# A 16-chunk mixer and expert kernel on one core: softmax, merge and scan of chunk 0 one unit down, weight pieces awaited one by one, chunk 1's x1 made in one step

## The chip, the cores and the metric

The kernel runs on 1 core of one Trainium2 chip. The metric is the device time of one execution in microseconds (us). Three runs of the kernel before took 1112.18, 1112.43 and 1113.23 us; the median is 1112.43 us.

## The reference

The input has 16 sequences of 512 tokens with 128 features. Everything is float32. With LN as a layer norm without weights:

```
x = x + LN(attn(LN(x)))            # attn: a diagonal state space model, 64 states
x = x + LN(ffn(LN(x)))             # ffn: 8 experts, all of them run for every token

attn(u):  Bu = u @ B_w.T
          h  = causal convolution of Bu with the powers of 64 eigenvalues of modulus 1
          y  = h @ C_w.T + D * u
ffn(x):   cw = softmax(x @ w_router) * softmax(x @ w_gating / 0.1), normed over the experts
          out = sum over e of cw[e] * ((silu(x @ w_gate[e]) * (x @ w_up[e])) @ w_down[e])   # F = 512
```

## The kernel before

**Tiling.** One sequence is a chunk. Its expert work is cut into 32 units `k`: unit `k` is block `b = k % 4` (128 of the 512 hidden features) of expert `e = k // 4`. For a unit TensorE makes `g` and `u` (gate and up), ScalarE the silu `gate` and a rounded copy `hid_hi`, VectorE the product `hid`, and VectorE or GpSimd the rest `hid_lo = hid - hid_hi` (GpSimd for `k % 4` in 1 and 3). Four units later TensorE makes the down product `y`. Each product is three matmuls on split numbers (high by high, high by low, low by high; function `exact`), so a unit is nine matmuls of 128x512. After an expert's fourth down product VectorE multiplies `y` by the weights of the tokens, `cw_b` (`weigh`, L1127), and GpSimd adds the parts (`add_part`).

**Order.** Each engine runs its own list of instructions in the order written. What an engine does beside a unit stands in tables (L44 to L58) that give the unit after which a step comes: `FIRST_X_AT` and `FIRST_Y_AT` are the steps that prepare chunk 1 inside chunk 0, `SECOND_X_AT` those for chunk 2, and `FIRST_OWN_AT` the softmax of chunk 0's own router. From chunk 1 on the tables `X_AT`, `Y_AT` and `OWN_AT` hold; the change leaves them alone.

**The mixer in chunk 0.** For chunk 1 the steps are: `lo_x` (`act_lo`, VectorE), `bu` (two matmuls into `m_ps`), `merge`, `enter_cos`, `enter_sin`, `scan` (a running sum over 512 tokens), `leave`, `fold`, `lo_w` (all VectorE), `c` (two matmuls), `y`, `turn_y` (four transposes on TensorE into `n_ps`), `stats_y`, `var_y`, then `z` and the residual, the second norm (`stats_x1`, `var_x1`, `scale_x1`), `turn_xe`, `lo_xe` and the router's `logits`.

**Waits around the change.** `u` of unit k waits for `hid` of unit k-2 (L506). The down product of expert 2, at unit 12, writes the `y` buffer of expert 0 and waits until `weigh` of expert 0 has read it (L520). `weigh` of expert 0 stands at unit 10 and needs `cw_b`, which comes by two DMAs from the last step of the softmax (`weights`, unit 6).

**Weights.** The 8 experts' weights come as three pieces each (gate, up, down; 24 pieces numbered n = 3e + i) into one of two stage slots, by SyncE's DMAs. ScalarE rounds a piece to `w_hi` (`round_piece`), and the rest `w_lo` is made for pieces 0 to 8 by TensorE and ScalarE before the loop (`make_lo`, `keep_lo`), for pieces 9 to 23 by GpSimd inside chunk 0 (`split_piece`) at the units in `LATE_SPLITS`. A slot is loaded again when all three pieces of the expert in it are split, and ScalarE waits for all three DMAs of an expert before it rounds the first piece. TensorE waits before an expert's first unit for all its three pieces.

Of the kernel before, what the change touches and what calls it, by code (L numbers as in the profile page):

```python
# [39 lines left out]
AHEAD = 3  # L40
PIECES = WCOLS // F

# [15 lines left out]
FIRST_OWN_AT = {"softmax": 1, "peak": 2, "silus": 3, "exps": 4, "products": 5, "weights": 6, "weigh": 10}  # L58
# [20 lines left out]
LATE_SPLITS = (3, 4, 5, 6, 7, 8, 9, 10, 11, 13, 14, 15, 19, 21, 22)  # L79
# [25 lines left out]
def build(nc, x_in, proj_in, angles_in, d_in, wgate_in, wup_in, wdown_in, out):  # L105
# [13 lines left out]
    with ExitStack() as ctx:  # L119
# [49 lines left out]
        y_shift = sb("y_shift", [P, NT])  # L169
# [20 lines left out]
        w_loaded = [sem("w_loaded0"), sem("w_loaded1")]  # L190
# [57 lines left out]
        def _(sp):  # L248
# [4 lines left out]

            def load_expert(e):
# [96 lines left out]
            for e in range(2, AHEAD):  # L351
                load_expert(e)
            load_expert(AHEAD)
            load_expert(AHEAD + 1)

            def body(c, par, first, last):
                if c + 2 < NCHUNK:
                    load_x(c + 2)
                if first:
                    load_expert(AHEAD + 2)  # L360
                store_cw(c, par)
                for e in range(E):
# [4 lines left out]
                    if e == 3 and first:  # L367
                        load_expert(AHEAD + 3)
# [3 lines left out]
                    if e == 5 and first:  # L372
                        load_expert(AHEAD + 4)
# [19 lines left out]
        def _(pe):  # L393
# [103 lines left out]

            def gate_up(c, par, k, first):
                e, b, buf = k // NB, k % NB, k % 2
                if first and b == 0:  # L500
                    if e < AHEAD:
                        pe.wait_ge(w_lo_act, PIECES * (e + 1))
                    else:
                        pe.wait_ge(w_lo_done, PIECES * (e + 1 - AHEAD))
# [7 lines left out]
            def down(c, k, first):  # L512
# [95 lines left out]
            def body(c, par, first, last):  # L608
                for k in range(UNITS):
# [991 lines left out]
```

## Time and profile before

| what | value |
|---|---|
| median of three runs | 1112.43 us |
| the profiled execution | 1113.27 us |
| its span in the trace | 1111.4 us |
| TensorE (PE) busy | 1094.8 us, 99% of the span |
| VectorE (DVE) busy | 941.4 us, 85% |
| ScalarE (ACT) busy | 744.6 us, 67% |
| GpSimd (POOL) busy | 719.2 us, 65% |
| chain that ended last | PE 88% of the span |

Times are counted from the span's start. PE is TensorE's matmuls and PEld its weight loads, DVE is VectorE, ACT ScalarE, POOL GpSimd, and SPq the queue on which SyncE issues DMAs. The loop over units starts at 26.54 us, chunk 1 at about 101 us. Successive matmuls overlap in the records, so the step between two starts, not the duration, is what one costs: 0.23 us for 128x512.

### The profile page before, as it was taken

The page shows a single profiled execution, that of the slowest core. Times are in us where ns is not written, and L with a number is a line of the kernel's source. Part 1 is how long each engine was busy: PE and PEld are TensorE (multiplying, and loading weights), DVE is VectorE, ACT ScalarE, POOL GpSimd, SP SyncE. Part 2 cuts the span into 40 slices and gives each one's busy share as a digit, 9 for nine tenths or more (in the row PEclk, how much of TensorE's full clock was granted, in tenths as well). Part 3 has the DMA queues.
Part 4 walks back from the last instruction along what each step waited for, and adds up shares of the span by engine and source line. Part 5 has one row for each costly group of instructions (what it writes and reads, how often), then busy time and mean ns, then how long its engine had stood idle before and what let it go on. Part 6 is the DMA issues. An engine that isn't in the chain of part 4 may idle for free.

```text
span 1111.4 us, 16965 instructions
## 1 busy us (share of the span) xinstructions
PE 1094.8 (99%) x4833; PEld 896.1 (81%) x4833; DVE 941.4 (85%) x1815; ACT 744.6 (67%) x1435; POOL 719.2 (65%) x886
## 2 busy tenths in 40 slices
PE   8899999999999999999999999999999999999997
PEld 5777888888888888888888888888888888888886
DVE  7999898897988979788897988979788897987866
ACT  5786676757667586676757667586676757666553
POOL 2785766748567575766748567575766748556454
PEclk9999999999999999999999999999999999999999
DMA  4430413313142221413213142221313213131110
GB/s 138 132 87 9 117 48 96 76 35 100 39 105 66 73 74 36 115 48 96 76 32 103 39 105 67 71 76 43 107 48 96 76 32 102 39 95 48 47 50 20
DMA packets 182285, 79.66 MB, mean 72 GB/s; under 512 B 124560, under 2 KB 160048, under 8 KB 182192
## 3 DMA queue, kind: packets, MB, share of 16 engines
q1 hardware_dynamic: 182192, 78.57, 26.5%
q8 instruction: 40, 0.66, 0.2%
q14 instruction: 53, 0.43, 0.1%
HBM read 59.14 MB, written 19.40 MB: 71 GB/s over the span
## 4 chain that ended last, share of the span: by engine, by line
PE 88%; issue 0%; POOL 0%; DVE 0%; POOLq 0%; ACT 0%; DVEq 0%; ACTq 0%
PE u L396 10%; PE g L397 10%; PE g L396 10%; PE u L397 10%; PE y L397 10%; PE y L396 10%; PE g L398 10%; PE u L398 10%; PE y L398 10%; PE n_ps L485 0%; PE n_ps L486 0%; PE m_ps L464 0%; PE m_ps L463 0%; PE m_ps L457 0%; PE m_ps L458 0%
## 5 line engine op out<-in xcount | busy, mean ns | idle before, releaser
L1500 POOL TENSOR_TENSOR hid_lo<-hid,hid_hi 128x512 fp32r<-128x512 f32 x256 | 341.0, 1332 | 306.6 <-ACT hid_hi L781 306.1
L775 ACT ACTIVATE gate<-g 128x512 f32<-128x512 f32 x512 | 306.0, 598 | 313.6 <-PE g L398 312.8
L1115 DVE TENSOR_TENSOR hid<-gate,u 128x512 f32<-128x512 f32 x512 | 348.0, 680 | 145.7 <-ACT gate L775 110.0
L781 ACT ACTIVATE hid_hi<-hid 128x512 fp32r<-128x512 f32 x512 | 319.6, 624 | 20.0 <-DVE hid L1115 19.3
L1124 DVE TENSOR_TENSOR hid_lo<-hid,hid_hi 128x512 fp32r<-128x512 f32 x256 | 218.4, 853 | 0.2
L396 PE MATMUL u<-xe_hi,w_hi 128*128 128x512 f32 (+1 forms) x516 | 201.0, 389 | 2.9 <-DVE hid L1115 2.7
L396 PE MATMUL g<-xe_hi,w_hi 128*128 128x512 f32 (+1 forms) x516 | 200.4, 388 | 0.3 <-DVE xe_lo L1251 0.3
L397 PE MATMUL g<-xe_lo,w_hi 128*128 128x512 f32 (+1 forms) x516 | 200.1, 388 | 0.0
L397 PE MATMUL u<-xe_lo,w_hi 128*128 128x512 f32 (+1 forms) x516 | 200.0, 388 | 0.0
L398 PE MATMUL u<-xe_hi,w_lo 128*128 128x512 f32 (+1 forms) x516 | 199.9, 387 | 0.0
L398 PE MATMUL g<-xe_hi,w_lo 128*128 128x512 f32 (+1 forms) x516 | 199.9, 387 | 0.0
L396 PE MATMUL y<-hid_hi,w_hi 128*128 128x512 f32 (+1 forms) x516 | 199.6, 387 | 0.0
L397 PE MATMUL y<-hid_lo,w_hi 128*128 128x512 f32 (+1 forms) x516 | 199.5, 387 | 0.0
L398 PE MATMUL y<-hid_hi,w_lo 128*128 128x512 f32 (+1 forms) x516 | 199.4, 387 | 0.0
L1507 POOL TENSOR_TENSOR acc<-acc,y_part 128x512 f32<-128x512 f32 x110 | 143.5, 1305 | 27.2 <-DVE y_part L1133 25.6
L396 PEld LDWEIGHTS u<-xe_hi,w_hi 128*128 128x128 f32 x516 | 96.9, 188 | 26.2 <-DVE hid L1115 6.5
L396 PEld LDWEIGHTS g<-xe_hi,w_hi 128*128 128x128 f32 x516 | 96.9, 188 | 20.9 <-ACT w_lo L658 0.9
L396 PEld LDWEIGHTS y<-hid_hi,w_hi 128*128 128x128 f32 x516 | 96.9, 188 | 20.3
L398 PEld LDWEIGHTS u<-xe_hi,w_lo 128*128 128x128 f32 x516 | 96.9, 188 | 20.0
L398 PEld LDWEIGHTS g<-xe_hi,w_lo 128*128 128x128 f32 x516 | 96.9, 188 | 19.9
L397 PEld LDWEIGHTS y<-hid_lo,w_hi 128*128 128x128 f32 x516 | 96.9, 188 | 19.8
L398 PEld LDWEIGHTS y<-hid_hi,w_lo 128*128 128x128 f32 x516 | 96.9, 188 | 19.7
(251 smaller groups left out, 1200.8 us busy)
## 6 DMA issues: line engine op xcount, KB each, us to landing
cw_b<-cw_scratch SPq DMA_DIRECT2D x128, 256.0 KB, 3.4
x_sb<-x_in SPq DMA_DIRECT2D x16, 256.0 KB, 3.2
out_scratch<-acc_t SPq DMA_DIRECT2D x60, 64.0 KB, 1.9
ffn<-out_scratch SPq DMA_DIRECT2D x15, 256.0 KB, 2.7
x_out<-o_sb SPq DMA_DIRECT2D x15, 256.0 KB, 2.2
xn_scratch<-mix_t SPq DMA_DIRECT2D x56, 64.0 KB, 2.2
feat<-xn_scratch SPq DMA_DIRECT2D x14, 256.0 KB, 2.6
y_scratch<-mix_t SPq DMA_DIRECT2D x56, 64.0 KB, 1.9
```

The source lines that it names most:

```text
L396: nc.tensor.matmul(dst, w_h, x_h, start=start, stop=False)
L397: nc.tensor.matmul(dst, w_h, x_l, start=False, stop=False)
L398: return nc.tensor.matmul(dst, w_l, x_h, start=False, stop=stop)
L775: nc.scalar.activation(gate[:, k % 2, :], g_ps[k % 2][:], ACT.Silu).then_inc(gate_ready, 1)
L781: nc.scalar.activation(hid_hi[:, slot(c, k), :], hid[:, slot(c, k), :], ACT.Copy).then_inc(hi_ready, 1)
L1115: nc.vector.tensor_tensor(hid[:, slot(c, k), :], gate[:, k % 2, :], u_ps[k % 2][:], ALU.mult).then_inc(hid_ready, 1)
L1124: nc.vector.tensor_tensor(hid_lo[:, slot(c, k), :], hid[:, slot(c, k), :], hid_hi[:, slot(c, k), :].bitcast(f32), ALU.subtract).then_inc(l ...
L1500: nc.gpsimd.tensor_tensor(hid_lo[:, slot(c, k), :], hid[:, slot(c, k), :], hid_hi[:, slot(c, k), :].bitcast(f32), ALU.subtract).then_inc(l ...
L1507: nc.gpsimd.tensor_tensor(acc[:, par, :], acc[:, par, :], y_part[:, e % 2, :], ALU.add).then_inc(part_added, 1)
```

## The change

Five things change.

1. In chunk 0, `products`, `weights` and `weigh` of expert 0 move one unit down (to 6, 7, 11), and so do `merge`, `enter`, `scan`, `leave`, `fold`, `lo_w`, `c`, `y` and `turn_y` of chunk 1; `bu` and `lo_x` stay. The statistics of chunk 2's x move from unit 5 to unit 7.
2. Chunk 1's x1 is made as in chunk 0: VectorE computes x + y * rstd per tile of 128 tokens straight out of `n_ps` (`first_residual`), and the part of the layer norm that shifts a token by a constant, which the second norm removes, is kept in `y_shift` and added in the last norm of chunk 1 (`fin_norms`). ScalarE's four instructions `z` and VectorE's `shift_y` go. The steps from the residual to `turn_xe` come one or two units earlier.
3. Weight pieces are awaited one by one: a piece's DMA waits for the same piece of the expert before in its slot, ScalarE waits for that piece's DMA, and TensorE waits for the gate, up and down piece each at its first use.
4. `LATE_SPLITS` is spread: every unit from 3 to 7, then every second one (9, 11, 13, 14, 15, 17, 19, 21, 23, 25).
5. Two semaphore counts follow, since `z_ready` is no longer raised in chunk 0.

```diff
-AHEAD = 3
+PE_PIECES = 9
...
-FIRST_X_AT = {"scale_x_a": 1, "scale_x_b": 2, "turn_x": 3, "hi_x": 4, "du": 4, "lo_x": 5, "bu": 7, "move_b": 7, "merge": 7, "enter_cos": 8, "enter_sin": 8, "scan": 9,
-              "leave": 10, "move_sines": 11, "fold": 11, "hi_w": 12, "lo_w": 12, "c": 14, "y": 15}
...
+FIRST_X_AT = {"scale_x_a": 1, "scale_x_b": 2, "turn_x": 3, "hi_x": 4, "du": 4, "lo_x": 5, "bu": 7, "move_b": 7, "merge": 8, "enter_cos": 9, "enter_sin": 9, "scan": 10,
+              "leave": 11, "move_sines": 12, "fold": 12, "hi_w": 13, "lo_w": 13, "c": 15, "y": 16}
...
-FIRST_OWN_AT = {"softmax": 1, "peak": 2, "silus": 3, "exps": 4, "products": 5, "weights": 6, "weigh": 10}
+FIRST_OWN_AT = {"softmax": 1, "peak": 2, "silus": 3, "exps": 4, "products": 6, "weights": 7, "weigh": 11}
...
-LATE_SPLITS = (3, 4, 5, 6, 7, 8, 9, 10, 11, 13, 14, 15, 19, 21, 22)
+LATE_SPLITS = (3, 4, 5, 6, 7, 9, 11, 13, 14, 15, 17, 19, 21, 23, 25)
...
             def load_expert(e):
-                if 2 <= e < AHEAD + 2:
-                    sp.wait_ge(w_lo_act, PIECES * (e - 1))
-                elif e >= AHEAD + 2:
-                    sp.wait_ge(w_lo_done, PIECES * (e - 1 - AHEAD))
                 s = e % 2
-                sp.dma_start(stage[:, s, 0:F], wgate_in[e]).then_inc(w_loaded[s], 16)
+                wait_staged(e, 0)
+                sp.dma_start(stage[:, s, 0:F], wgate_in[e]).then_inc(w_loaded[s][0], 16)
...
             def round_piece(e, i):
-                if i == 0:
-                    act.wait_ge(w_loaded[e % 2], 48 * (e // 2 + 1))
+                act.wait_ge(w_loaded[e % 2][i], 16 * (e // 2 + 1))
...
             def first_residual():
-                dve.wait_ge(z_ready, 1)
-                nc.vector.tensor_tensor(x1[:, 1], x_sb[:, 1], x1[:, 1], ALU.add).then_inc(x1_ready, 1)
+                dve.wait_ge(rstd_ready, 6)
+                shifts(y_shift[:, 1], mv, rstd).then_inc(shift_ready, 1)
+                for j in range(NT):
+                    last = nc.vector.scalar_tensor_tensor(out=x1[:, 1, j, :], in0=n_ps[:, j * P:(j + 1) * P],
+                                                          scalar=rstd[:, j:j + 1], in1=x_sb[:, 1, j, :],
+                                                          op0=ALU.mult, op1=ALU.add)
+                last.then_inc(x1_ready, 1)
```

The first place is VectorE's list in units 9 to 11 of chunk 0. Before (`sum_sb<-v_sb` is the scan, `acc<-y,cw_b` the `weigh` of expert 0, `m_ps<-sum_sb,trig` is `leave`):

```order
L1115 TENSOR_TENSOR hid<-gate,u 128x512
L1124 TENSOR_TENSOR hid_lo<-hid,hid_hi 128x512
L974 SCALAR_TENSOR_TENSOR sum_sb<-v_sb 128x512
L1115 TENSOR_TENSOR hid<-gate,u 128x512
L1133 TENSOR_TENSOR acc<-y,cw_b 128x512
L978 TENSOR_TENSOR m_ps<-sum_sb,trig 128x512
```

Now, from the `hid` of unit 10 on:

```order
L1125 TENSOR_TENSOR hid<-gate,u 128x512
L988 SCALAR_TENSOR_TENSOR sum_sb<-v_sb 128x512
L1125 TENSOR_TENSOR hid<-gate,u 128x512
L1134 TENSOR_TENSOR hid_lo<-hid,hid_hi 128x512
L1143 TENSOR_TENSOR acc<-y,cw_b 128x512
L992 TENSOR_TENSOR m_ps<-sum_sb,trig 128x512
```

The scan has moved behind the `hid` of unit 10, and the `weigh` of expert 0 behind the `hid` and a `hid_lo` of unit 11.

The second place is VectorE's list in units 5 and 6 (`pr`, `gsum`, `psum_` and `den` are `products`, `act_lo` is what `bu` waits for). Before:

```order
L1056 TENSOR_TENSOR pr<-lg 128x32
L1057 TENSOR_REDUCE gsum<-lg 128x8
L1060 TENSOR_REDUCE psum_<-pr 128x4
L1061 TENSOR_TENSOR den<-gsum 128x4
L957 TENSOR_TENSOR act_lo<-n_ps,act_hi 128x512
L875 BN_STATS stats<-x_sb 128x6 x4
L1115 TENSOR_TENSOR hid<-gate,u 128x512
```

Now:

```order
L971 TENSOR_TENSOR act_lo<-n_ps,act_hi 128x512
L1125 TENSOR_TENSOR hid<-gate,u 128x512
L1066 TENSOR_TENSOR pr<-lg 128x32
L1067 TENSOR_REDUCE gsum<-lg 128x8
L1070 TENSOR_REDUCE psum_<-pr 128x4
L1071 TENSOR_TENSOR den<-gsum 128x4
```

The softmax step stood ahead of `act_lo` and of the `hid` of unit 6, and now stands behind both.

The third place is VectorE's list in units 20 to 22, where chunk 1's x1 is made. Before (`x1` is printed as `x`):

```order
L1115 TENSOR_TENSOR hid<-gate,u 128x512
L923 TENSOR_TENSOR x<-x_sb,x 128x512
L875 BN_STATS stats<-x 128x6 x4
L961 TENSOR_TENSOR m_ps<-m_ps,sum_sb 64x512
L1115 TENSOR_TENSOR hid<-gate,u 128x512
```

Now:

```order
L1143 TENSOR_TENSOR y_part<-y,cw_b 128x512
L912 SCALAR_TENSOR_TENSOR y_shift<-mv,rstd 128x4
L934 SCALAR_TENSOR_TENSOR x<-n_ps,rstd,x_sb 128x128 x4
L1125 TENSOR_TENSOR hid<-gate,u 128x512
L1134 TENSOR_TENSOR hid_lo<-hid,hid_hi 128x512
L884 BN_STATS stats<-x 128x6 x4
L1125 TENSOR_TENSOR hid<-gate,u 128x512
```

One addition of 128x512 in unit 22 has become four instructions of 128x128 in unit 20, and the statistics stand in unit 21.

## Rows read from the trace of the kernel before

**Rows 1.** Busy time by stretch: the stretch, its length, then each engine.
```profile
42.36:56.84 14.48, 11.18 (x46) 7.99 (x45) 14.26 (x26) 8.08 (x15) 13.20 (x16) 1.00 0.59 183
...
56.84:66.97 10.13, 9.76 (x42) 7.36 (x42) 9.92 (x15) 9.82 (x20) 8.47 (x6) 1.00 0.19 45
...
82.00:97.00 15.00, 13.73 (x61) 10.36 (x60) 14.83 (x30) 11.57 (x23) 10.40 (x8) 1.00 0.01 2
97.00:120.00 23.00, 22.61 (x99) 18.31 (x100) 19.75 (x50) 11.89 (x24) 10.12 (x11) 1.00 0.25 65
120.00:1080.00 960.00, 960.00 (x4234) 791.98 (x4233) 815.49 (x1492) 651.23 (x1251) 634.71 (x807) 1.00 0.27 70
```

**Rows 2.** Waits of PE from 40 to 130: us in total, times, longest.
```profile
PE u L396 <- DVE hid L1115: 2.7, 5, 1.5
```

**Rows 3.** Timeline of PE: start, us, what, and the idle time before it.
```profile
43.64 0.47 PE L457 MATMUL m_ps<-act_hi,proj_hi 128*128 128x512 f32 x1 [1.28 <-DVE act_lo L957]
...
56.84 0.39 PE L396 MATMUL y<-hid_hi,w_hi 128*128 128x512 f32 x1
...
66.97 0.66 PE L403 MATMUL n_ps<-ident,y_sb 128*128 128x128 f32 x4 [0.37 <-DVE y_sb L992]
...
96.98 0.39 PE L485 MATMUL n_ps<-xe_hi,router 128*32 128x512 f32 x1 [0.79 <-issue]
```

**Rows 4.** Timeline of DVE, units 5 to 10 of chunk 0.
```profile
40.40 1.28 DVE L1056 TENSOR_TENSOR pr<-lg 128x32 f32<-128x32 f32 x1
...
41.95 0.94 DVE L1061 TENSOR_TENSOR den<-gsum 128x4 f32<-128x4 f32 x1
42.81 0.68 DVE L957 TENSOR_TENSOR act_lo<-n_ps,act_hi 128x512 fp32r<-128x512 f32 x1
...
47.28 1.59 DVE L1124 TENSOR_TENSOR hid_lo<-hid,hid_hi 128x512 fp32r<-128x512 f32 x1
...
53.10 2.31 DVE L974 TENSOR_TENSOR_SCAN sum_sb<-v_sb 128x512 f32<-128x512 f32 x1
55.33 0.66 DVE L1115 TENSOR_TENSOR hid<-gate,u 128x512 f32<-128x512 f32 x1
55.91 0.68 DVE L1133 TENSOR_TENSOR acc<-y,cw_b 128x512 f32<-128x512 f32 x1
```

**Rows 5.** Timeline of POOL beside the scan.
```profile
52.83 1.50 POOL L1500 TENSOR_TENSOR hid_lo<-hid,hid_hi 128x512 fp32r<-128x512 f32 x1 [0.20 <-ACT hid_hi L781]
```

**Rows 6.** Timeline of DVE, the head, and units 20 to 28.
```profile
24.50 0.34 DVE L1239 SCALAR_TENSOR_TENSOR x<-g,rstd,x_sb 128x128 f32<-128x128 f32 x1
...
25.98 0.42 DVE L1251 TENSOR_TENSOR xe_lo<-n_ps,xe_hi 128x256 fp32r<-128x256 f32 x1
...
77.14 0.69 DVE L1115 TENSOR_TENSOR hid<-gate,u 128x512 f32<-128x512 f32 x1 [1.22 <-ACT gate L775]
...
81.68 0.84 DVE L923 TENSOR_TENSOR x<-x_sb,x 128x512 f32<-128x512 f32 x1
...
90.43 1.22 DVE L974 TENSOR_TENSOR_SCAN sum_sb<-v_sb 128x512 f32<-128x512 f32 x1
...
93.80 0.68 DVE L1124 TENSOR_TENSOR hid_lo<-hid,hid_hi 128x512 fp32r<-128x512 f32 x1
...
96.20 0.67 DVE L1017 TENSOR_TENSOR xe_lo<-n_ps,xe_hi 128x512 fp32r<-128x512 f32 x1
```

**Rows 7.** Waits of all engines from 66 to 98.
```profile
DVE hid L1115 <- ACT gate L775: 2.1, 4, 1.2
```

**Rows 8.** Timeline of ACT: two roundings that waited for a DMA.
```profile
21.76 1.15 ACT L653 ACTIVATE w_hi<-stage 128x512 fp32r<-128x512 f32 x2 [0.58 <-DMA stage<-wdown_in]
...
75.38 0.63 ACT L653 ACTIVATE w_hi<-stage 128x512 fp32r<-128x512 f32 x1 [0.86 <-DMA stage<-wdown_in]
```

**Rows 9.** The scan's line over the whole trace: min/median/max in ns.
```profile
L974 DVE TENSOR_TENSOR_SCAN sum_sb<-v_sb x15: 1216/1890/2308, 53.1 to 950.8; 128x512 f32<-128x512 f32 x15
```

**Rows 10.** DVE's `hid_lo`, grouped, 40.4 to 97: count, busy us, mean ns.
```profile
L1124 DVE TENSOR_TENSOR hid_lo<-hid,hid_hi 128x512 fp32r<-128x512 f32 x12 | 12.4, 1031 | 0.1
```

More of the change, by code:

```diff
@@ L189, in build @@
         x_loaded = [sem("x_loaded0"), sem("x_loaded1")]
-        w_loaded = [sem("w_loaded0"), sem("w_loaded1")]
+        w_loaded = [[sem(f"w_loaded{s}_{i}") for i in range(PIECES)] for s in range(2)]
         w_hi_done, w_lo_done = sem("w_hi_done"), sem("w_lo_done")
@@ L350, in _ @@
             load_x(1)
-            for e in range(2, AHEAD):
+            for e in range(2, 5):
                 load_expert(e)
-            load_expert(AHEAD)
-            load_expert(AHEAD + 1)
             def body(c, par, first, last):
@@ L496, in turn_out_last, with wait_piece @@
                 nc.tensor.transpose(u_ps[0][:, P:2 * P], acc[:, par, 3 * P:], ident[:]).then_inc(fin_turned, 1)
+            def wait_piece(e, i):
+                n = PIECES * e + i
+                if n < PE_PIECES:
+                    pe.wait_ge(w_lo_act, n + 1)
+                else:
+                    pe.wait_ge(w_lo_done, n + 1 - PE_PIECES)
             def gate_up(c, par, k, first):
                 e, b, buf = k // NB, k % NB, k % 2
[L500 to L504, printed above, removed]
                 for dst, off, used, done in ((g_ps[buf], 0, gate_ready, g_done), (u_ps[buf], F, hid_ready, u_done)):
@@ L507, in gate_up @@
                         pe.wait_ge(used, UNITS * c + k - 1)
+                    if first and b == 0:
+                        wait_piece(e, off // F)
                     cols = slice(off + b * P, off + (b + 1) * P)
@@ L518, in down @@
                     pe.wait_ge(lo_dve, N_DVE_LO * c + lo_count(k))
+                if first and b == 0:
+                    wait_piece(e, 2)
                 if b == 0 and not (first and e < 2):
@@ L728, in mix_z @@
                 for j in tiles:
-                    src = n_ps[:, j * P:(j + 1) * P] if c == 1 else y_tok[:, j, :]
-                    last = nc.scalar.activation(x1[:, c % X1S, j, :], src, ACT.Identity,
+                    last = nc.scalar.activation(x1[:, c % X1S, j, :], y_tok[:, j, :], ACT.Identity,
                                                 bias=shift[:, j:j + 1], scale=rstd[:, j:j + 1])
@@ L902, in shifts @@
             def shifts(dst, m, r):
-                return nc.vector.scalar_tensor_tensor(out=dst[:], in0=m[:, :, 0], scalar=-1.0, in1=r[:],
+                return nc.vector.scalar_tensor_tensor(out=dst, in0=m[:, :, 0], scalar=-1.0, in1=r[:],
                                                       op0=ALU.mult, op1=ALU.mult)
@@ L1242, in keep_shift @@
             def keep_shift(tiles):
-                return nc.vector.scalar_tensor_tensor(out=y_shift[:, tiles], in0=mv[:, tiles, 0], scalar=-1.0,
+                return nc.vector.scalar_tensor_tensor(out=y_shift[:, 0, tiles], in0=mv[:, tiles, 0], scalar=-1.0,
                                                       in1=rstd[:, tiles], op0=ALU.mult, op1=ALU.mult)
@@ L1356, in body @@
                             first_var(1)
-                        if k == at.get("shift_y"):
-                            shift_y(1)
                         if k == at.get("var_x1"):
```

54 lines of the change are left out of this document (30 added, 24 removed).

## The prediction

> **What bounds the kernel now.** I read the busy time by stretch first. From 120 to 1080 us TensorE is busy all 960.00 us, so nothing that leaves its matmuls alone can help there; the change touches no table of those chunks. What can be won lies in chunk 0 and just behind it: TensorE stands idle 3.30 us of 42.36 to 56.84, 0.37 to 66.97, 1.27 of 82 to 97 and 0.39 of 97 to 120, together 5.33 us [rows 1]. The reader is to see in the same rows that VectorE is busy 14.26 of 14.48 us in the first of these stretches: it sets the pace there, and TensorE waits for it. The list of TensorE's waits has 2.7 us in five waits of `u` for `hid` [rows 2]; its timeline has the rest: 1.28 us of `bu` for `act_lo`, 0.37 us of `turn_y` for `y`, 0.79 us before the logits [rows 3]. The wait before the logits is put down to nothing, but `xe_lo` ends at 96.20 + 0.67 = 96.87 and the logits start at 96.98, so it is `xe_lo` [rows 3, 6]. Last the timelines, for which of VectorE's instructions lie ahead of each awaited one.
>
> A row of VectorE also shows how long it is held up. The scan took 2.31 us from 53.10, and ended 1.08 us after GpSimd's `hid_lo`, which ran from 52.83 to 54.33; the scan at 90.43 took 1.22 us; `hid_lo` takes 0.68 us free and 1.59 us at 47.28 [rows 4 to 6]. So a VectorE instruction that reads two SBUF tensors waits for the end of the GpSimd instruction under way, then runs at its free time. The Trainium skill (SBUF — State Buffer, SBUF: two separate sides) says the same: VectorE and GpSimd share a port pair that the first holds for its whole instruction. It adds that a VectorE instruction with only one SBUF input, at ordinary speed, is exempt; by it the four new instructions below, which read PSUM and one SBUF tensor, cost their free time, and if it didn't hold here they would wait for one GpSimd instruction, up to 1.5 us by the row of GpSimd, and the sum would be +0.7.
>
> **1. Units 5 to 12: the wait of `bu` goes, and the `weigh` of expert 0 is next.** `act_lo` ended at 43.49 and now stands ahead of `products`, so it ends near 40.40 + 0.68 = 41.1, before TensorE's 42.36. That saves 1.28 us of wait [rows 3, 4]. But TensorE then only runs ahead to the next thing VectorE owes it. The down product of expert 2 at unit 12 started at 56.84, right behind the `weigh` of expert 0, which ended at 55.91 + 0.68 = 56.59 [rows 3, 4]. VectorE had no idle time from 40.40 to there, and its list up to `weigh` keeps every instruction and gains the `hid` of unit 11 (step 0.6 us) and a `hid_lo` (0.6 us free, 1.3 behind a GpSimd instruction). Traced, each two-input instruction waiting for GpSimd's instruction of that moment, I get against before: `products` -0.9 (one of the two hold-ups at 40.40 and 41.95 goes), the first `hid_lo` -0.3, the last step of the softmax +0.75 (GpSimd's split now lies beside it), the second `hid_lo` +0.2, the scan -0.8, `hid` +0.6, the added `hid_lo` +1.3. Sum +0.85 us: `weigh` ends near 57.4 and the down product starts near 57.45, 0.6 us later than before. The bounds are -1.2 us (no hold-ups left on the scan and the two `hid_lo`: 1.1 + 0.9 + 0.5 less than before, 1.3 added) and +2.0 us (the same hold-ups as before, 1.9 added). I take +0.6. TensorE's waits at `bu` and at `u` of units 8 to 12 come back as one wait of about 3 us before this down product. `cw_b` doesn't bind: `weights` ends about 1 us later, near 47.6, and its copies land by about 54.
>
> **2. Units 13 to 17: `y` in time.** `turn_y` now stands one unit behind `y`'s own move, and by the same tracing VectorE has caught up: its wait of 0.37 us goes, with about 0.1 us of slow restart behind it [rows 3]. -0.5 us. Bounds: 0 and -0.5. After unit 17 the kernel stands at +0.1.
>
> **3. Units 18 to 29: VectorE's account up to `xe_lo`.** From 80 us VectorE is again behind: `u` waits twice (0.5 us) and the logits 0.8 us; with the restarts TensorE loses 1.8 us here. What decides is when `xe_lo` ends, the last of an unbroken row. VectorE was idle 2.1 us in 66 to 98, in four waits for `gate`, the longest 1.22 us at 77.14 behind ScalarE, which had itself waited 0.86 us for the last piece of expert 7 [rows 6 to 8]. ScalarE now rounds the first pieces as they land and has lost four instructions, and x1 and its statistics, 1.7 us, stand in units 20 and 21, where this idle time was. I let 1.9 us of the idle time be filled, and 0.3 us come back at units 17 and 18, where VectorE no longer lags. The four 128x128 instructions cost 4 x 0.27 = 1.1 us (step between two such, row at 24.50) where the addition took 0.8: +0.3. The scan of unit 25 ran free at 1.22 us; the median scan of the trace takes 1.89 [rows 6, 9]. GpSimd now has a piece to split at units 23 and 25, beside it, where it had one at 22; I charge half the difference, since it may still run free: +0.35. Account: -1.9 + 0.3 + 0.3 + 0.35 = -0.95, taken as -0.9. Bounds: -1.8 (all that TensorE loses here) and +1.2 (a full hold-up of 1.1 us on the scan and one on a `hid_lo` of 0.9 more, with only 0.8 of the idle time filled).
>
> **4. What is hidden.** In the head ScalarE's 0.58 us wait for expert 2's last piece goes. But the first unit waits for `xe_lo` at 25.98, which follows VectorE's own unbroken list: 0, bounds -0.3 and 0 [rows 6, 8]. The per-piece waits on SyncE hold nothing long: piece 14 is split at unit 9, near 52, behind the four `cw_b` copies, and the next copy waits for `weigh` anyway. TensorE's waits for pieces: the latest split, unit 25, is for a down product of unit 32. The 0.39 us of idle time near 117 hangs on a load of x behind the copy of `y`, which keeps its place: 0. GpSimd's extra addition in chunk 1 is 128x4: 0.
>
> **Sum.** +0.6 - 0.5 - 0.9 = -0.8 us. The profiled execution took 1113.27 us (span 1111.4), so a like one would take 1112.5 (span 1110.6); the median of the runs, 0.84 us below it, becomes 1111.6.
>
> **Rivals.**
> *A, the `weigh` of expert 0 binds harder.* The hold-ups stay as they were, the two instructions are added in full, and the down product of unit 12 starts 2.0 us later. It becomes slower than before from the point where this exceeds what 2 and 3 give back, 1.4 us; since later steps are then late too, I count only 0.7 back: +1.3, 1113.7 us. For it: VectorE had no gap in this stretch. Against: GpSimd has two splits fewer in units 8 to 11. Chance 0.19.
> *B, the collisions thin out.* With GpSimd's pieces in every second unit the scan and both `hid_lo` of units 7 to 11 run free, step 1 comes to -1.2 and step 3 to -1.3; with -0.5 that is -3.0, 1109.4 us. For it: 12 `hid_lo` took 1031 ns in the mean against 680 free, so 4.2 us of hold-ups in them alone leave room [rows 10]. Against: the number of GpSimd's instructions is the same. Chance 0.20.
> *C, nothing is won.* VectorE's work is the same, each wait that goes turns up at the next instruction that VectorE owes, and the logits start where they did: 1112.4 us. Chance 0.21.
> *My forecast*, 1111.6 with its own range 1110.8 to 1112.3: chance 0.40.
>
> **How the numbers follow.** A measurement of this kernel tells some 0.2%, 2.2 us, from no change. Faster by that needs B nearly whole (0.18 of its 0.20) and a tail of mine (0.01): 0.19. Slower by that is A at its far end: 0.05. The rest, 0.76, is within. The range reaches into B and over most of A: 1109.2 to 1113.6. No more than all of TensorE's idle time, 1107.1, can be had.
>
> **What would show it.** Right: no wait at `bu`; one wait of 2.5 to 3.5 us before the down product of unit 12, with `weigh` of expert 0 ending just ahead of it, near 57.4; no wait at `turn_y`; the logits near 96. Wrong: that down product before 56 (then B), or after 58.5 (A); a `u` that waits more than 1 us in units 24 to 28 because the scan of unit 25 took over 2 us; or ScalarE waiting over 0.5 us for a piece at units 19 to 25.

## The result, and the profile after

The changed kernel took 1115.07 us in the median of 20 runs (1113.32 to 1117.06), the kernel before 1112.97 us beside it (20 runs). The ratio is 1.0016, 95% interval [1.0009, 1.0022]: slower by 0.16%, which lies within the 0.2% that the prediction calls no change, but outside its range of times. The profiled execution took 1116.99 us (span 1115.2), 3.7 us more than that of before (1113.27, span 1111.4). It is the slowest but one of the twenty, 1.9 us above their median, so its stretches probably show more loss than a typical execution has.

First the busy time by stretch of the changed kernel: stretch and length, then PE, PEld, DVE, ACT, POOL, the granted clock, the DMA share and GB/s.

```profile
42.36:56.84 14.48, 10.10 (x44) 7.68 (x42) 14.26 (x25) 8.42 (x16) 11.77 (x15) 1.00 0.47 141
56.84:66.97 10.13, 9.61 (x35) 7.79 (x36) 9.08 (x12) 6.91 (x13) 8.13 (x7) 0.83 0.16 44
82.00:97.00 15.00, 13.47 (x60) 10.37 (x60) 14.86 (x27) 10.04 (x20) 9.68 (x7) 1.00 0.00 1
97.00:120.00 23.00, 21.85 (x96) 17.32 (x94) 18.69 (x43) 12.24 (x24) 10.26 (x8) 1.00 0.15 37
120.00:1080.00 960.00, 958.70 (x4227) 790.90 (x4228) 816.40 (x1499) 650.59 (x1250) 632.72 (x805) 1.00 0.27 71
...
58.00:60.00 2.00, 2.00 (x7) 1.56 (x6) 2.00 (x4) 1.64 (x4) 1.87 (x2) 0.55 0.41 139
60.00:62.00 2.00, 2.00 (x6) 1.55 (x6) 1.18 (x3) 1.88 (x4) 1.42 (x2) 0.59 0.00 0
```

Two things answer to [rows 1]. TensorE is idle 4.38 us of the first stretch where it was 3.30, and the granted clock of 56.84 to 66.97 is 0.83 where it was 1.00: from 58 to 62 us TensorE ran near the lower of its two levels, 1.2 of 2.4 GHz. All else that is lost lies ahead of 122 us; behind it `u` of each unit starts a constant 3.81 us later than before.

TensorE's waits from 20 to 130 us (us in total, times, longest):

```profile
PE u L401 <- DVE hid L1125: 5.4, 3, 2.4
PE y L401 <- DVE acc L1143: 2.5, 1, 2.5
PE g L401 <- ACT w_lo L668: 0.6, 1, 0.6
PE n_ps L490 <- issue: 0.6, 1, 0.6
```

`bu` and `turn_y` are gone from the list, as predicted. In their place stand two long waits where before none was over 1.52 us [rows 2]. TensorE's timeline has them, and what follows the second:

```profile
49.80 0.50 PE L401 MATMUL u<-xe_hi,w_hi 128*128 128x512 f32 x1 [2.39 <-DVE hid L1125]
...
57.37 0.47 PE L401 MATMUL y<-hid_hi,w_hi 128*128 128x512 f32 x1 [2.51 <-DVE acc L1143]
...
58.13 0.55 PE L401 MATMUL g<-xe_hi,w_hi 128*128 128x512 f32 x1
58.48 0.63 PE L402 MATMUL g<-xe_lo,w_hi 128*128 128x512 f32 x1
58.91 0.63 PE L403 MATMUL g<-xe_hi,w_lo 128*128 128x512 f32 x1
...
61.78 0.40 PE L401 MATMUL g<-xe_hi,w_hi 128*128 128x512 f32 x1
...
94.95 0.50 PE L401 MATMUL u<-xe_hi,w_hi 128*128 128x512 f32 x1 [1.16 <-DVE hid L1125]
...
99.32 0.40 PE L490 MATMUL n_ps<-xe_hi,router 128*32 128x512 f32 x1 [0.63 <-issue]
...
121.30 0.50 PE L401 MATMUL u<-xe_hi,w_hi 128*128 128x512 f32 x1 [1.82 <-DVE hid L1125]
```

The reader is to see the step from one matmul's start to the next: 0.23 us at 57.67, then 0.43 us from 58.48 on. The nine steps from 58.13 to 61.78 took 3.65 us where nine of 0.23 take 2.1: the slow stretch cost 1.6 us. The logits start at 99.32, not at 96.98 [rows 3], and there is a `u` at 121.30 that waits 1.82 us.

VectorE's timeline, to be laid beside [rows 4, 6]:

```profile
53.47 1.53 DVE L988 TENSOR_TENSOR_SCAN sum_sb<-v_sb 128x512 f32<-128x512 f32 x1
...
56.54 0.68 DVE L1143 TENSOR_TENSOR acc<-y,cw_b 128x512 f32<-128x512 f32 x1
...
76.00 1.79 DVE L971 TENSOR_TENSOR act_lo<-feat,act_hi 128x512 fp32r<-128x512 f32 x1
...
78.98 1.11 DVE L934 SCALAR_TENSOR_TENSOR x<-n_ps,rstd,x_sb 128x128 f32<-128x128 f32 x4
...
90.27 1.81 DVE L1134 TENSOR_TENSOR hid_lo<-hid,hid_hi 128x512 fp32r<-128x512 f32 x1
92.00 2.32 DVE L988 TENSOR_TENSOR_SCAN sum_sb<-v_sb 128x512 f32<-128x512 f32 x1
...
98.53 0.68 DVE L1027 TENSOR_TENSOR xe_lo<-n_ps,xe_hi 128x512 fp32r<-128x512 f32 x1
...
119.79 0.87 DVE L884 BATCH_NORM_STATS2 stats<-x_sb 128x6 f32<-128x128 f32 x4 [3.21 <-DMA x_sb<-x_in]
```

`weigh` of expert 0 ends at 57.22, the down product behind it starts at 57.37. The second scan, 1.22 us before, now takes 2.32, and the `hid_lo` ahead of it 1.81. GpSimd's timeline shows what lies beside them:

```profile
70.99 1.69 POOL L1446 TENSOR_TENSOR w_lo<-stage,w_hi 128x512 fp32r<-128x512 f32 x1
...
75.92 1.32 POOL L1446 TENSOR_TENSOR w_lo<-stage,w_hi 128x512 fp32r<-128x512 f32 x1
...
90.24 1.29 POOL L1446 TENSOR_TENSOR w_lo<-stage,w_hi 128x512 fp32r<-128x512 f32 x1
91.48 1.75 POOL L1508 TENSOR_TENSOR hid_lo<-hid,hid_hi 128x512 fp32r<-128x512 f32 x1
```

From 70 to 92 us, at units 17 to 25 of its table, GpSimd splits five pieces (two more, at 80.32 and 85.23, are left out here); before it split three (units 19, 21 and 22). The reader is to see the chain at the end. The piece ended at 91.53, and VectorE's `hid_lo`, which takes 0.68 us free, ended 0.55 us later; GpSimd's own `hid_lo`, which stood behind the piece, ended at 93.23, and the scan, 1.22 us free, ended 1.09 us later.

To compare kernels I use the start of `u` of a unit in TensorE's timeline, against the kernel before. Unit 4 is the reference point, because its start differs between executions of one kernel: in some, before included, the granted clock is 0.83 from 10 to 20 us, in others 1.00, and those start unit 4 some 1.1 us earlier. Net of that, the changed kernel lost 1.61 us in units 4 to 20, 0.97 in 20 to 38 and 1.43 in 38 to 40, together 4.01.

### The profile page after: what moved, and what is told of

It reads as the page before. It is cut to its first block, busy times and chain, and to the rows that moved or that the text cites. A ratio compares the mean times of both kernels' runs of the same rounds, so it can differ in the third digit from the quotient of the medians.

```text
span 1115.2 us, 16976 instructions
## 1 busy us (share of the span) xinstructions
PE 1094.5 (98%) x4833; PEld 897.5 (80%) x4833; DVE 943.7 (85%) x1818; ACT 743.2 (67%) x1431; POOL 719.6 (65%) x887
## 4 chain that ended last, share of the span: by engine, by line
PE 88%; issue 0%; POOL 0%; DVE 0%; POOLq 0%; ACT 0%; DVEq 0%; ACTq 0%
PE u L401 10%; PE g L402 10%; PE u L402 10%; PE g L403 10%; PE u L403 10%; PE y L402 10%; PE g L401 10%; PE y L403 10%; PE y L401 10%; PE n_ps L490 0%; PE n_ps L491 0%; PE m_ps L469 0%; PE m_ps L468 0%; PE m_ps L463 0%; PE m_ps L462 0%
## 5 line engine op out<-in xcount | busy, mean ns | idle before, releaser
L402 PEld LDWEIGHTS u<-xe_lo,w_hi 128*128 128x128 f32 x516 | 97.0, 188 | 19.8
```

The lines of the kernel that those rows point to most:

```text
L402: nc.tensor.matmul(dst, w_h, x_l, start=False, stop=False)
```

## The experiments

The table has all runs: the median with its range and number, the ratio to the kernel before on the same chip, the profiled execution, and the loss (+) or gain (-) by stretch against the trace of before, net of the head as above. e1 to e4, e5 to e8 and e9 to e12 ran on one chip each, where the kernel before took 1113.10, 1112.21 and 1112.03 us, so between groups only the ratios can be compared, and these to some 0.1% (1 us).

```
                            median (range), n            ratio  [95%]            profiled  4-20  20-38  38-40   sum
after                       1115.07 (1113.32-1117.06) 20  1.0016 [1.0009,1.0022]  1116.99  +1.61  +0.97  +1.43  +4.01
e1_weigh10                  1116.72 (1115.18-1117.81)  9  1.0029 [1.0019,1.0039]  1115.26  +0.84  +1.71  +0.64  +3.20
e2_warm                     1114.17 (1113.34-1115.73) 11  1.0011 [1.0002,1.0020]  1114.17   0.00  +1.29  +0.75  +2.04
e3_x1_as_before             1113.66 (1112.69-1118.03) 11  1.0010 [0.9998,1.0021]  1112.83  +0.03  +0.81  -0.05  +0.79
e4_x_load_early             1113.36 (1112.67-1114.92) 11  1.0003 [0.9994,1.0012]  1112.67  +0.04  +1.24  -0.68  +0.60
e5_last_splits              1113.67 (1112.76-1114.78) 11  1.0013 [1.0004,1.0022]  1114.77  +1.62  -0.11  -0.02  +1.49
e6_last_splits_x_early      1112.84 (1111.42-1113.98) 11  1.0004 [0.9995,1.0013]  1112.87  +1.59  -0.09  -0.68  +0.82
e7_before_x_early           1111.31 (1111.10-1112.79) 11  0.9992 [0.9983,1.0000]  1112.38   0.00  +0.18  -0.68  -0.49
e8_x1_alone                 1113.05 (1112.06-1115.39) 11  1.0013 [1.0004,1.0022]  1112.42  -0.58  +0.91  -0.11  +0.22
e9_warm_both                1111.62 (1111.45-1112.78) 11  0.9991 [0.9980,1.0001]  1112.78  -0.04  +0.24  -0.68  -0.48
e10_tables_alone            1114.65 (1114.20-1116.87) 11  1.0018 [1.0007,1.0029]  1114.50  +0.42  +0.65   0.00  +1.07
e11_pieces_x_early          1110.88 (1110.66-1111.82) 11  0.9990 [0.9981,0.9999]  1111.79  +0.04  -0.67  -0.68  -1.31
e12_x1_pieces_x_early       1110.25 (1110.01-1111.26) 11  0.9984 [0.9975,0.9992]  1111.09  -0.56  -0.68  -0.68  -1.92
```

### 1. Is it the place of `weigh`?

```
-FIRST_OWN_AT = {... "products": 6, "weights": 7, "weigh": 11}
+FIRST_OWN_AT = {... "products": 6, "weights": 7, "weigh": 10}
```

> The changed kernel, with the weigh of expert 0 back at unit 10, so right behind the hid of unit 10 and ahead of the scan. Theory one (the late weigh makes TensorE stand still for 2.5 us before the down product of unit 12, and the clock halves behind it): the down product starts near 54.7 instead of 57.37, no stretch of 56 to 64 us has a granted clock under 1.0, and the time falls by 2.5 to 3.5 us against the changed kernel, to about 1112.3. Rival (VectorE's total work decides, the wait only moves to the u of unit 13 or 14): the down product starts early but a wait of 2 us or more follows within two units, the clock may still halve, and the time falls by less than 1 us.

1116.72 us, 1.0029 [1.0019, 1.0039]: not faster than the changed kernel, which both halves of the expectation had it be. Its timeline of TensorE:

```profile
48.90 0.50 PE L401 MATMUL u<-xe_hi,w_hi 128*128 128x512 f32 x1 [2.41 <-DVE hid L1125]
56.00 0.50 PE L401 MATMUL u<-xe_hi,w_hi 128*128 128x512 f32 x1 [0.69 <-DVE hid L1125]
59.33 0.50 PE L401 MATMUL u<-xe_hi,w_hi 128*128 128x512 f32 x1 [1.00 <-DVE hid L1125]
63.88 0.47 PE L468 MATMUL m_ps<-act_hi,proj_hi 128*128 128x512 f32 x1 [0.75 <-DVE act_hi L1001]
```

The wait of 2.51 us before the down product is gone and stands again, in three pieces of 2.44 us together, at the next results that VectorE owes. VectorE's sum of work sets the pace here, not the place of one step. The granted clock stayed at 1.00, and still units 4 to 20 lost 0.84 us: among other things the scan, now at 53.17, took 2.19 us where it took 1.53 in the changed kernel.

### 2. Is it the clock behind a long wait?

In the second kernel nine matmuls whose result nobody reads are issued in the second wait:

```
+                if first and k == 8:
+                    for i in range(9):
+                        nc.tensor.matmul(n_ps[:], minus[:], xe_hi[:, 0, :], start=True, stop=True)
```

> The changed kernel, with nine extra matmuls of 128x512 into an unused buffer ahead of the down product of unit 12, inside the 2.5 us in which TensorE waits for the weigh. Nothing that is waited for comes earlier. Theory one (1.6 us of the loss is the clock that halves after this wait): the down product still starts near 57.4, the next eight matmuls step by 0.23 us instead of 0.43, and the time falls by 1 to 1.8 us in executions that had the halved clock. Rival (the clock is halved by something else, or TensorE then only waits longer for VectorE in units 13 to 17): granted clock still 0.83 in 56.84 to 66.97, or the saved time turns up as a wait before unit 18; less than 0.4 us.

```profile
48.95 0.50 PE L401 MATMUL u<-xe_hi,w_hi 128*128 128x512 f32 x1 [2.40 <-DVE hid L1128]
56.46 0.50 PE L401 MATMUL y<-hid_hi,w_hi 128*128 128x512 f32 x1 [0.35 <-DVE acc L1146]
```

The clock is 1.00 throughout, and units 4 to 20 come out even with before: 0.00 where the changed kernel lost 1.61. The medians don't tell this: 1.0011 [1.0002, 1.0020] overlaps the changed kernel's 1.0016 [1.0009, 1.0022]. And not all of the 1.6 us is kept, since units 20 to 38 now lose 1.29 where the changed kernel lost 0.97: at unit 38 the two stand at +1.29 and +2.58, so the slow clock was worth 1.3 us there. It is one cause of several. The first long wait, left unfilled here, was not followed by a slow clock in this trace, as in the changed kernel. The last of the experiments on this (e9) has the splits of experiment 4 and the load of experiment 3 as well, these nine matmuls, and eight more in the first long wait:

```
+                    if first and k == 10 and off:
+                        for i in range(8):
+                            nc.tensor.matmul(n_ps[:], minus[:], xe_hi[:, 0, :], start=True, stop=True)
```

> The kernel of the run before with split units 19 to 22 and the early load of x, and extra matmuls inside both long waits of TensorE: eight ahead of the u of unit 10 (a wait of 2.4 us), nine ahead of the down product of unit 12 (2.5 us). Theory one (after a wait of 2.4 us or more the clock sometimes halves for about 3 us, and a half-rate stretch behind the second wait costs 1.6 us): no stretch of 44 to 64 us under 1.0, the upper cluster of times of that run (1113.6 to 1114.0) is gone, the median falls by 0.5 to 1.4 us to 1111.4 to 1112.3. Rival (the spread comes from the head alone): the same clusters as without the extra matmuls.

```profile
50.08 0.50 PE L403 MATMUL u<-xe_hi,w_hi 128*128 128x512 f32 x1 [0.56 <-DVE hid L1133]
57.58 0.50 PE L403 MATMUL y<-hid_hi,w_hi 128*128 128x512 f32 x1 [0.39 <-DVE acc L1151]
```

1111.62 us (0.9991) against 1112.84 (1.0004) for e6, which differs in the seventeen matmuls alone. The two were not timed side by side, and the intervals of their ratios overlap. Their traces differ as those of e2 and the changed kernel do: -0.04 against +1.59 in units 4 to 20, and +0.20 against +1.50 at unit 38. Every run lists the mean granted clock of its execution: in e9 eight of eleven have 0.998 or 0.999 and lie within 1111.45 to 1111.71; in e6 four have 0.998 and none more. The slow stretch in the head lowers that mean as well, so by itself it doesn't say which of the two an execution had.

### 3. The load of x behind the copy of `y`, and x1

```
             def body(c, par, first, last):
-                if c + 2 < NCHUNK:
+                if c + 2 < NCHUNK and c != 1:
                     load_x(c + 2)
...
+                if first:
+                    load_x(3)
```

> The changed kernel, with the load of chunk 3's x issued ahead of the store and load of chunk 2's y at the end of chunk 0, instead of behind them. Theory one (VectorE's wait for this load at unit 4 of chunk 1, 3.2 us in the changed kernel and 1.6 before, costs TensorE 1.8 and 0.4 us): the wait of u near 121 us goes, and the time falls by 0.5 us where y's store lands as before and by up to 1.9 us where it lands late. Rival (y_tok comes as late and VectorE waits there, one unit on): the wait moves to the statistics of y and the time is the same within 0.3 us.

`u` no longer waits near 121 us: units 38 to 40 gain 0.68 on before, where the changed kernel lost 1.43. 1113.36 us in the median, in groups: five runs at 1112.67 to 1112.71 with a mean clock of 0.997, four at 1114.87 to 1114.92 with 0.995 or 0.996. In its profiled execution the slow stretch came behind the first long wait, not the second:

```profile
48.00:50.00 2.00, 1.11 (x3) 0.92 (x4) 2.00 (x6) 1.13 (x3) 1.34 (x7) 0.76 0.08 23
50.00:52.00 2.00, 2.00 (x6) 1.52 (x6) 1.95 (x5) 1.03 (x3) 1.92 (x3) 0.50 0.79 265
```

```profile
48.89 0.68 PE L403 MATMUL u<-xe_hi,w_hi 128*128 128x512 f32 x1 [2.40 <-DVE hid L1127]
56.48 0.47 PE L403 MATMUL y<-hid_hi,w_hi 128*128 128x512 f32 x1 [0.94 <-DVE acc L1145]
```

There it costs nothing (+0.04): TensorE would have waited for `acc` anyway, and the 1.6 us come off that wait, 0.94 where it is 2.51. So the same slow stretch costs 1.6 us in one place and nothing in the other, and in which an execution has it differs.

The same load moved in the kernel before:

> The kernel before, with the load of chunk 3's x issued ahead of the store and load of chunk 2's y. Theory: VectorE's wait of 1.56 us and TensorE's of 0.39 us at unit 6 of chunk 1 go, so the time falls by 0.4 to 0.6 us. Rival (the time there is set by y_tok): same within 0.2 us.

1111.31 us, 0.9992 [0.9983, 1.0000], with 0.68 gained in units 38 to 40: this wait was there to be had without the change (by the trace; the interval of the ratio reaches to no difference).

x1 put back to the form of before, all else as changed:

```
             def first_residual():
-                dve.wait_ge(rstd_ready, 6)
-                ... four scalar_tensor_tensor 128x128 from n_ps
+                dve.wait_ge(z_ready, 1)
+                nc.vector.tensor_tensor(x1[:, 1], x_sb[:, 1], x1[:, 1], ALU.add).then_inc(x1_ready, 1)
```

> The changed kernel, with chunk 1's x1 made as before (ScalarE's z, one addition on VectorE, steps at the units of the kernel before, only turn_y, its statistics and variance one unit down). Theory one (the new x1 was worth its idle time, and the loss of 1 us in units 18 to 29 comes from GpSimd's pieces at units 23 and 25 beside hid_lo and scan): the logits stay at 99 or later, since the pieces are still there, and the time is the same or up to 1 us longer. Rival (the four instructions out of PSUM and the earlier statistics are what delays VectorE): the logits come 0.8 us or more earlier and the time falls by about 1 us.

1113.66 us, 1.0010 [0.9998, 1.0021]: not slower than the changed kernel. Units 20 to 38 lose 0.81 with the old x1. The traces to set beside it are e2 and e4, since there too unit 20 is level with before (0.00 and +0.04): with the new x1 they lose 1.29 and 1.24. So in this surrounding x1's new form costs 0.4 to 0.5 us in the traces and brings nothing; the medians don't tell. The other way round, the new x1 in the kernel before, with its old splits and its one wait for all three pieces; with it `turn_y` and the statistics of y move one unit down:

```
-FIRST_Y_AT = {... "rstd_y": 18, "shift_y": 19, "z_a": 20, "z_b": 21, "own_residual": 22, "stats_x1": 22, ...}
+FIRST_Y_AT = {... "rstd_y": 18, "own_residual": 20, "stats_x1": 21, ...}
```

> The kernel before with only the new x1 (four instructions out of PSUM in unit 20, statistics in unit 21, turn_y, its statistics and variance one unit down); softmax, merge and scan, the piece waits and the split units as before. Theory one (it is hidden or helps while no piece lies beside the scan): the logits at 96.98 or up to 1 us earlier, the time the same or up to 1 us less. Rival (the new x1 is a cause of its own of the loss in units 18 to 29): the logits later by 0.4 us or more.

```profile
76.19 0.69 DVE L1120 TENSOR_TENSOR hid<-gate,u 128x512 f32<-128x512 f32 x1 [2.14 <-ACT gate L779]
```

1113.05 us, 1.0013 [1.0004, 1.0022]. VectorE's list gets shorter, but ScalarE holds it: it waits 2.53 us for the last piece of an expert, and VectorE 2.14 us for the gate behind it, where before it was 1.22 [rows 6]. The idle time was only handed on. The gain of 0.58 in units 4 to 20 is that of the later `turn_y`, which waits no more.

### 4. The pieces split late

```
-LATE_SPLITS = (3, 4, 5, 6, 7, 9, 11, 13, 14, 15, 17, 19, 21, 23, 25)
+LATE_SPLITS = (3, 4, 5, 6, 7, 9, 11, 13, 14, 15, 17, 19, 20, 21, 22)
```

> The changed kernel, with the last four of GpSimd's pieces split at units 19, 20, 21 and 22 instead of 19, 21, 23 and 25; all else as changed. Theory one (the piece at unit 25 holds up the hid_lo and the scan of unit 25 by 1.1 us each, and with them xe_lo and the logits): the scan of unit 25 takes 1.2 to 1.3 us instead of 2.3, the logits come 1.2 to 2.2 us earlier, and the time falls by 1.2 to 2 us. Rival (some other GpSimd instruction, hid_lo or the addition, lies beside the scan then, or VectorE is held up earlier instead): the logits come less than 0.5 us earlier.

```profile
91.44 0.68 DVE L1134 TENSOR_TENSOR hid_lo<-hid,hid_hi 128x512 fp32r<-128x512 f32 x1
92.04 1.22 DVE L988 TENSOR_TENSOR_SCAN sum_sb<-v_sb 128x512 f32<-128x512 f32 x1
```

Both run free: 0.68 where it was 1.81, 1.22 where it was 2.32. Units 20 to 38 go from +0.97 to -0.11. The piece split at unit 25 was what held them, the `hid_lo` directly and the scan through GpSimd's `hid_lo` behind it. Of the 2.2 us that the two rows gave back, 1.08 reach TensorE, since others are held now beside GpSimd's instructions: `mv<-stats` took 1.14 us at 83.75 (0.16 in the changed kernel), `m_ps<-sum_sb` 1.15 at 93.75 (0.68). The median, 1113.67 us, is 1.0013 [1.0004, 1.0022] of before, which can't be told from the changed kernel's 1.0016: the gain is seen in the trace alone. The rest of the loss, 1.6 us, is the clock: 0.78, 0.50 and 0.87 from 58 to 64 us. With the early load of x too:

> The changed kernel with both: the last four pieces at units 19 to 22, and the load of chunk 3's x ahead of chunk 2's y store. If the two causes are separate, it is faster than the changed kernel by the sum, 2.5 to 3.5 us, so 1112.0 or a little under, and within 0.5 us of the kernel before; what is left over it is then the clock that halves in some executions. If they share a cause, it is no better than the better of the two alone.

1112.84 us, 1.0004 [0.9995, 1.0013]. Of the 4.0 us lost 0.8 is left: the 1.6 behind the second long wait, less the 0.68 of the early load and 0.09. Again the traced clock fell, to 0.50 and 0.72 from 58 to 62 us. Against e4 (1.0003), which has the early load but not the new splits, the median gained nothing that can be told.

### 5. The parts by themselves

The kernel before with only the tables that move softmax, merge and scan:

```
-... "merge": 7, "enter_cos": 8, "enter_sin": 8, "scan": 9, "leave": 10, ... "y": 15}
+... "merge": 8, "enter_cos": 9, "enter_sin": 9, "scan": 10, "leave": 11, ... "y": 16}
-FIRST_OWN_AT = {... "exps": 4, "products": 5, "weights": 6, "weigh": 10}
+FIRST_OWN_AT = {... "exps": 4, "products": 6, "weights": 7, "weigh": 11}
```

> The kernel before with only the tables changed: softmax, merge and scan and all behind them one unit down, statistics of chunk 2's x at unit 7; x1, piece waits and split units as before. Theory one (this part alone makes the two long waits of TensorE, wins nothing without the clock's fall and loses 1.6 us with it): two waits of 2.3 us or more at the u of unit 10 and the down product of unit 12, no wait at bu and turn_y, unit 20 within 0.3 us of the kernel before from the head on or 1.6 us later with halved clock; time the same to 1.2 us longer. Rival (the tables win 1 us or more, and the other parts lose it): unit 20 earlier by 0.8 us or more, time 1 us shorter.

```profile
50.00:52.00 2.00, 1.75 (x6) 1.38 (x7) 2.00 (x5) 1.77 (x4) 1.67 (x6) 0.85 0.19 67
52.00:54.00 2.00, 2.00 (x6) 1.61 (x5) 1.96 (x4) 1.37 (x3) 1.92 (x3) 0.50 0.90 319
```

1114.65 us, 1.0018 [1.0007, 1.0029]: some 2 us slower than before, where 1.2 us at most was expected. The slow clock is there, behind a wait of 2.40 us at 50.24; as in e4 most of its cost comes off the second wait, which is 0.92 us at 57.83. In units 20 to 38 another 0.65 us are lost without a late piece: ScalarE waited 2.50 us for an expert's last piece at 76.72 (before 0.86), as in e8, and VectorE 3.2 us in all for gates. This part alone makes the kernel as slow, by the median, as the whole change does. The kernel before with only the waits for single pieces, and the early load of x (its splits and tables as before); then the same with the new x1:

```
             def load_expert(e):
-                if 2 <= e < AHEAD + 2:
-                    sp.wait_ge(w_lo_act, PIECES * (e - 1))
...
+                wait_staged(e, 0)
                 sp.dma_start(stage[:, s, 0:F], wgate_in[e]).then_inc(w_loaded[s][0], 16)
+                wait_staged(e, 1)
...
             def round_piece(e, i):
+                act.wait_ge(w_loaded[e % 2][i], 16 * (e // 2 + 1))
```

> The kernel before with the waits piece by piece and the early load of x; tables, split units and x1 as before. Theory one (ScalarE's wait of 0.86 us at unit 19 and VectorE's wait of 1.2 to 1.4 us behind it go, VectorE gets that far ahead, and part of the waits of units 26, 27 and the logits goes): 0.3 to 1.2 us faster than the kernel before with the early load alone, so about 1110.4 to 1111.0. Rival (GpSimd's instructions fall beside VectorE's instead, or the wait is hidden): no more than 0.2 us from 1111.3.

> The kernel before with the new x1, the waits piece by piece and the early load of x; softmax, merge and scan and the split units as before. Theory one (x1 alone lost 0.9 us in units 20 to 29 because VectorE first waited 2.1 us for ScalarE's late piece at unit 20; without that wait its work lies in idle time and turn_y's wait of 0.5 us is saved too): 1109.8 to 1110.8. Rival (the four instructions are plain added work on a full VectorE): 1111.3 or later.

```profile
43.47 0.47 PE L464 MATMUL m_ps<-act_hi,proj_hi 128*128 128x512 f32 x1 [1.20 <-DVE act_lo L973]
...
55.86 0.50 PE L403 MATMUL u<-xe_hi,w_hi 128*128 128x512 f32 x1 [1.52 <-DVE hid L1127]
```

1110.88 us (0.9990 [0.9981, 0.9999]) and 1110.25 us (0.9984 [0.9975, 0.9992]). The second beats both kernels. It keeps the short waits of before in units 7 to 12 (the two between these rows are 0.17 and 0.36 us) and the clock at 1.00 there; VectorE's idle time from 66 to 98 us is 0.8 us (before 2.1), and the second scan runs free (1.22 us at 89.02). With the pieces awaited singly the new x1 no longer loses in units 20 to 38 (-0.68, with the old x1 -0.67; in e8 +0.91). What e12 has over e11 is 0.6 us in units 4 to 20, the wait at the later `turn_y`, and the medians differ by as much (1110.88 and 1110.25, side by side), though their intervals overlap.

## Why the prediction was wrong, point by point

Against the -0.8 of the sum the traced losses are +4.01. Of the 4.8 us between them 1.5 lie in steps 1 and 2, where the slow clock had no term, 1.9 in step 3 and 1.4 in step 4.

**Step 1, +0.6: right in mechanism and end, in part by luck, and incomplete in effect.** The wait of `bu` went; `weigh` ended at 57.22 (57.4 predicted), the down product started at 57.37 (57.45 predicted). But the "one wait of about 3 us" came as two, of 2.39 and 2.51 us, and the sum had no term for the clock behind a long wait. Rows show it: behind the second, TensorE took up to 0.43 us a matmul over 3.65 us and lost 1.6. Where the matmuls of e2 and e9 fill the wait, units 4 to 20 come out at 0.00 and -0.04, against the "+0.1" of the prediction: steps 1 and 2 were right but for this term.

That `weigh` came out so near, +0.82 where the hand trace had +0.85, is in part luck: its terms missed and cancelled. The last step of the softmax took 1.9 us more than before, not 0.75, since two of its small instructions were held up, which took 0.15 and 0.19 us before:

```profile
44.46 1.24 DVE L1076 SCALAR_TENSOR_TENSOR den<-den,psum_ 128x4 f32<-128x4 f32 x1
...
45.95 1.03 DVE L1082 TENSOR_TENSOR v_sb<-pr,den 128x32 f32<-128x32 f32 x1
```

Against it the second `hid_lo` lost 0.5 where +0.2 was said, `products` lost 1.1 for 0.9, and the added `hid_lo` cost 1.0 for 1.3. Rival A rested on the same place, but with `weigh` 2 us late, which it was not.

**Step 2, -0.5: right.** `turn_y` runs at 70.44 with no wait before it, and where it moved while the softmax and the scan stayed (e8, e12) units 4 to 20 gain 0.58 and 0.56.

**Step 3, -0.9: this is the step that failed worst.** It came to +0.97, and to +1.29 and +1.24 in e2 and e4, where TensorE did not reach unit 20 late. VectorE's account from the `hid` of unit 17 to the end of `xe_lo`, from its timeline, is 27.77 us before (69.10 to 96.87) and 29.20 after (70.01 to 99.21):

```
                                            before   after   difference   predicted
idle, waiting for a gate                      1.90    0.20      -1.70     -1.9 + 0.3
x1 in four instructions and y_shift, for one  0.87    1.10      +0.23     +0.3
statistics of y, moved into the stretch       0.00    0.88      +0.88      none
held up: hid_lo of unit 24                    0.60    1.73      +1.13   }
held up: the scan                             1.14    2.24      +1.10   }
held up: act_lo of chunk 1                    0.68    1.71      +1.03   } +0.35
all else                                     22.58   21.34      -1.24   }
sum                                          27.77   29.20      +1.43
```

The idle time was filled as predicted, and x1 cost what was said. The failed term is the +0.35 for hold-ups: the last four rows come to +2.02. I had charged "half the difference" of a median scan for one piece beside it, and left out that every second unit up to 25 puts five pieces into units 17 to 25 where three were, each a GpSimd instruction of 1.3 us or more. Beside four of the five a VectorE instruction is held up: `act_lo` at 76.00, `hid_lo` at 80.61, `shift` at 85.87, `hid_lo` at 90.27. The statistics of y, 0.88 us, had no term either. e5 shows the part of the last piece: without it at unit 25 the scan and the `hid_lo` run free, and the stretch comes to -0.11. But with TensorE in time at unit 20 and the same splits (e9) it is +0.24, still 1.1 us from the -0.9; VectorE has no idle time left there, and which of its instructions would have to go was not tested. What the prediction named as its refutation is there: a `u` that waits over 1 us (1.16 at 94.95) because the second scan took over 2. The upper bound, +1.2, was made of just this pair; it held in the changed kernel's trace, and not in those of e1, e2 and e4 (+1.71, +1.29, +1.24). That the four new instructions run free beside GpSimd's addition at 79.06 (1.11 us for the four at 78.98) excludes the wait of up to 1.5 us, and with it the sum of +0.7, that the prediction weighed. By the exemption for one SBUF input in the Trainium skill (SBUF — State Buffer, SBUF: two separate sides) that is how it should be, and the trace agrees.

**Step 4, 0: wrong by 1.4 us in the profiled execution.** The load of x "keeps its place" in SyncE's queue, but stands behind a wait for the store of `y`:

```profile
110.91 2.11 SPq L286 DMA_DIRECT2D y_scratch<-mix_t  x4
116.23 0.38 SPq L332 DMA_DIRECT2D y_tok<-y_scratch  x1
116.65 0.51 SPq L252 DMA_DIRECT2D x_sb<-x_in  x1
```

The stores were issued at 110.91 (before 108.53), as late as everything else, but SyncE then waited 3.2 us for their landing (before 1.4), so x came at 119.79, and VectorE stood idle 3.21 us. The slowest of the four stores took 3.8 us to land, before 2.7. The loss goes with that landing: e1 and e2, with 3.1 and 3.4 us, lost 0.64 and 0.75 here, and e3, e5 and e10, with 2.6 to 2.7, nothing. Why the landing differs is open. That the load's place is the cause of the wait is shown, by e4 and e7. For the head step 4 holds: no loss there.

**The rivals.** None had the clock in it. C was right in its core: what went at `bu` came back at the next thing owed (e1 shows it twice over). B was excluded by the rows above.

**How the median goes with it.** The three losses add up to 4.0 us in the one profiled execution; the medians differ by 2.1. The mean granted clock that each run lists is 0.998 or 0.999 in 29 of the 33 runs of before beside e9 to e12, 0.995 to 0.997 in all 20 of the changed kernel, and 0.998 or 0.999 again in seven of the eleven of e12. So some slow stretch more is in nearly every execution of the changed kernel; where it lies, and so what it costs, only the traces say. How much each of the other two causes weighs in a typical execution is open: the ratios of e4 and e6 (1.0003, 1.0004) lie 1.0 to 1.4 us below those of the changed kernel and e5, as the early load would have it, and for the late pieces they show nothing.

## What to carry to other kernels

Before an early result is moved ahead to take away a short wait, ask where the engine stops next: here several waits of up to 1.5 us cost only their length, while the same idle time in waits of 2.4 and 2.5 us was followed in six of eight traces by a clock near half for over 3 us. Where another engine sets the pace, moving its steps changes the place of the wait and not its sum; filling its idle time, or keeping off what holds it up, does, and for that all the neighbour's large instructions in the stretch are to be counted, each at the full hold-up. A load that stands in a queue behind a wait for a store is only as early as the slowest landing, so it belongs ahead of that wait if its buffer is free.

## What was not expected of the hardware

- Behind idle times of TensorE of 2.40 and 2.51 us (busy before them, at a clock of 1.00) the granted clock fell to 0.50 to 0.6 for some 3 us, while TensorE was busy without a gap; then it was 1.00 again. It followed the wait of 2.51 us in all three traces that have it unfilled (the changed kernel, e5, e6), and the wait of 2.39 to 2.41 us in three of eight (e3, e4, e10, not the changed kernel, e1, e2, e5, e6). No trace here has it from 26 to 1080 us behind a wait of 1.82 us or less.
- Seventeen matmuls that nobody reads, in the waits (nine in e2), cost nothing that can be seen: the next awaited one started 0.35 to 0.56 us after the last of them, at full clock.
- A hold-up takes small instructions too: the 128x4 `den` took 1.24 us at 44.46 in the changed kernel, and its `shift` 1.25 us at 85.87, where e5's took 0.15.
- Of four stores of the same size the slowest took 2.7, 3.1 and 3.8 us to land in three executions that issued them alike (before, e1, the changed kernel).
